# Both halves of a gated recurrence in one instruction each of tanh, decay, relu, gate, product and scan

## What is computed

```python
# recurrence: 256 inner features
hidden, gate = split(xn @ W_hg, 2)
z = sigmoid(gate);  a = 1 - z
h[t] = a[t] * h[t-1] + z[t] * (relu(hidden[t]) + 0.5)     # along each sequence
s = h @ W_out
# mixture of experts: a shared expert, and the best 2 of 16 routed ones
g = silu(shared(xn) + sum_k p_k * expert_k(xn))
out = x + s * g
```

## Time and profile before

| | us |
|---|---|
| median of 3 runs | 362.05 |
| the three runs | 361.15, 362.05, 365.03 |
| profiled execution, first to last instruction | 361.3 |
| TensorE busy | 304.3 (84%) |
| VectorE busy | 253.6 (70%) |
| ScalarE busy | 242.5 (67%) |
| GpSimd busy | 210.6 (58%) |

### The profile page before, as it was taken

The page is one execution under the profiler, slowest core; times in us unless marked ns, Lnnn a source line. Parts: engine busy times, 40 slices in busy tenths (PEclk is TensorE's granted clock), DMA queues, the critical chain, the costliest instruction groups (busy, mean ns, idle before and its releaser), DMA issues.

```text
span 361.3 us, 6017 instructions
## 1 busy us (share of the span) xinstructions
PE 304.3 (84%) x1532; PEld 197.9 (55%) x1532; DVE 253.6 (70%) x635; ACT 242.5 (67%) x518; POOL 210.6 (58%) x243
## 2 busy tenths in 40 slices
PE   0899999999979999995019879999999999999810
PEld 0457777766646666664015545656566666656510
DVE  7399999979998989795003457676767677676830
ACT  2789999988954788982026556767676776767410
POOL 4987544420137873777765646565656656565671
PEclk9999999999989999999557999999999999999975
DMA  8999996910003368333479624544645555520000
GB/s 241 289 406 412 416 437 236 427 66 0 3 22 133 135 225 324 114 150 138 156 239 402 263 86 124 173 130 131 184 151 147 149 146 153 150 76 17 15 0 1
DMA packets 27984, 63.82 MB, mean 177 GB/s; under 512 B 3701, under 2 KB 22784, under 8 KB 27056
## 3 DMA queue, kind: packets, MB, share of 16 engines
q1 hardware_dynamic: 20880, 45.78, 37.0%
q0 software_dynamic: 6784, 17.06, 12.7%
q10 hardware_dynamic: 288, 0.60, 0.5%
HBM read 29.52 MB, written 35.21 MB: 179 GB/s over the span
## 4 chain that ended last, share of the span: by engine, by line
PE 43%; issue 14%; POOL 14%; DVE 9%; ACT 8%; DMA 7%; another core or an unknown queue 2%; POOLq 0%; ACTq 0%; SPq 0%; DVEq 0%
PE p_u L976 13%; POOL slots L335 11%; PE p_u L903 8%; PE p_s L1001 8%; DMA slots<-arena,pos 5%; PE p_sh L988 3%; PE p_s L914 3%; PE p_lg L884 3%; ACT arena L444 2%; DVE rec L788 2%; PE p_xt L952 2%; POOL out L341 2%; DVE rec L780 1%; PE p_sh L923 1%
## 5 line engine op out<-in xcount | busy, mean ns | idle before, releaser
L341 POOL DMA_INDIRECT out<-arena x84 | 90.5, 1078 | 56.4 <-issue 40.1
L903 PE MATMUL p_u<-xT,w_front 128*128 128x512 f32 x192 | 92.3, 616 | 1.1 <-ACT xT L400 0.7
L335 POOL DMA_INDIRECT slots<-arena,pos x64 | 71.6, 1119 | 35.7 <-issue 17.9
L976 PE MATMUL p_u<-arena 128*128 x168 | 81.1, 606 | 0.0
L780 DVE TENSOR_TENSOR rec<-p_u,rec 128x512 f32<-128x512 f32 x42 | 29.0, 692 | 65.5 <-PE p_u L976 27.0
L1001 PEld LDWEIGHTS p_s<-arena,rec 128*128 128x128 f32 x336 | 40.9, 191 | 39.0 <-issue 38.9
L1001 PE MATMUL p_s<-arena,rec 128*128 x336 | 48.2, 286 | 6.7 <-ACT rec L464 3.0
L903 PEld LDWEIGHTS p_u<-xT,w_front 128*128 128x128 f32 x192 | 34.6, 195 | 33.5 <-issue 32.1
L444 ACT ACTIVATE arena<-arena 128x128 f32<-128x128 f32 x84 | 36.3, 480 | 14.8 <-DMA arena<-slots 14.8
L976 PEld LDWEIGHTS p_u<-arena 128*128 128x128 f32 x168 | 29.4, 196 | 20.7 <-issue 20.7
L543 DVE TENSOR_TENSOR_SCAN rec<-rec 128x512 f32<-128x512 f32 x32 | 39.2, 1225 | 1.1
(11 more groups left out here) (130 smaller groups left out, 433.0 us busy)
## 6 DMA issues: line engine op xcount, KB each, us to landing
slots<-arena SPq DMA_DIRECT2D x4, 4116.0 KB, 27.3
arena<-slots SPq DMA_DIRECT2D x42, 392.0 KB
arena<-in_W_lines SPq DMA_DIRECT2D x2, 2304.0 KB
arena<-in_x SPq DMA_DIRECT2D x16, 256.0 KB, 5.3
arena<-in_W_lines SPq DMA_DIRECT2D x1, 3072.0 KB
out<-arena POOLq DMA_INDIRECT x84
slots<-arena,pos POOLq DMA_INDIRECT x64
w_front<-in_W_front ACTq DMA_DIRECT2D x1, 392.0 KB, 3.5
```

Of the source, the lines that this page charges most:

```text
L335: pool.indirect_dma_start(slots, index, xrow[:, t], None).then_inc(s_disp[t % WINDOW], 16)
L341: pool.indirect_dma_start(out, index, xg[:, n % RX, h, X], None, bounds_check=T - 1, oob_is_err=False)\
L903: nc.tensor.matmul(p_u[:, n % 4], w_front[:, UPS[q]:UPS[q] + P], xT[:, c % XB], start=True, stop=True)\
L976: last = nc.tensor.matmul(p_u[:, n % 2 * 2 + h], xsT[:, n % 2, h * P:(h + 1) * P], w_lines[:, bass.DynSlice(line_at[2 * n + h], 4 * P)], s ...
```

## The change

The two halves of the inner features are handled together. `rec_in(c, j)`, called twice, becomes `rec_gates(c)` (tanh, then the decay a, each of both halves, 1024 columns) and `rec_hidden(c)` (relu, then the gate z). `rec_scan(c)` makes one product and one scan over 1024 columns; the zero decay at the start of each of the now four sequences still separates them. The projections are made in the order gate 0, gate 1, hidden 0, hidden 1, so that the two gates and the two hiddens lie in adjacent banks. The semaphores that counted halves count chunks. Nothing else changes.

```diff
@@ -223,7 +223,7 @@
 
         CONSTS = 17
         OFF_HG, OFF_S = E, E + 4 * P
-        UPS = [OFF_HG + 2 * P, OFF_HG, OFF_HG + 3 * P, OFF_HG + P, OFF_S, OFF_S + P]
+        UPS = [OFF_HG + 2 * P, OFF_HG + 3 * P, OFF_HG, OFF_HG + P, OFF_S, OFF_S + P]
 
         FIRST_TILES = FREE_CHUNKS * TT
         BLANK_BY_DVE = SLOTS // 8
@@ -399,21 +399,26 @@
                     act.wait_ge(s_up, NUP * (c - XB + 1))
                 nc.scalar.activation(xT[:, c % XB], p_xt[:, :], ACT.Copy).then_inc(s_xTe, 1)
 
-            def rec_in(c, j):
-                n = NH * c + j
-                act.wait_ge(s_up, NUP * c + 2 * j + 1)
+            def both(c, q):
+
+                return p_u[:, (NUP * c + q) % 4:(NUP * c + q) % 4 + NH]
+
+            def rec_gates(c):
+                act.wait_ge(s_up, NUP * c + 2)
                 if c >= 1:
-                    act.wait_ge(s_v, n - 1)
-                nc.scalar.activation(rec_z[:, j], p_u[:, (NUP * c + 2 * j) % 4], ACT.Tanh, scale=0.5).then_inc(s_tanh, 1)
-                act.wait_ge(s_up, NUP * c + 2 * j + 2)
+                    act.wait_ge(s_v, c)
+                nc.scalar.activation(rec_z, both(c, 0), ACT.Tanh, scale=0.5).then_inc(s_tanh, 1)
+                act.wait_ge(s_tanh, c + 1)
                 if c >= 1:
-                    act.wait_ge(s_scan, n - 1)
-                nc.scalar.activation(rec_v[:, j], p_u[:, (NUP * c + 2 * j + 1) % 4], ACT.Relu).then_inc(s_relu, 1)
-                act.wait_ge(s_tanh, n + 1)
-                halves = lambda a: a[:, j].rearrange("p (q n) -> p q n", q=2)[:, :, 1:]
+                    act.wait_ge(s_scan, c)
+                halves = lambda a: a.rearrange("p j (q n) -> p (j q) n", q=2)[:, :, 1:]
                 nc.scalar.activation(halves(rec_a), halves(rec_z), ACT.Copy, bias=0.5, scale=-0.5).then_inc(s_a, 1)
-                act.wait_ge(s_a, n + 1)
-                nc.scalar.activation(rec_z[:, j], rec_z[:, j], ACT.Copy, bias=0.5, scale=0.5).then_inc(s_z, 1)
+
+            def rec_hidden(c):
+                act.wait_ge(s_up, NUP * c + 2 * NH)
+                nc.scalar.activation(rec_v, both(c, NH), ACT.Relu).then_inc(s_relu, 1)
+                act.wait_ge(s_a, c + 1)
+                nc.scalar.activation(rec_z, rec_z, ACT.Copy, bias=0.5, scale=0.5).then_inc(s_z, 1)
 
             def shared_silu(c):
                 act.wait_ge(s_up, NUP * c + 5)
@@ -474,10 +479,10 @@
                 normalise(c)
             act.wait_ge(s_wfront, 16)
             for i in range(NCH):
-                rec_in(i, 0)
+                rec_gates(i)
                 for c in read(i)[:-1]:
                     copy_xT(c)
-                rec_in(i, 1)
+                rec_hidden(i)
                 for c in read(i)[-1:]:
                     copy_xT(c)
                 shared_silu(i)
@@ -530,18 +535,18 @@
                 nc.vector.tensor_copy(lg[:, a * TT:b * TT].rearrange("p t e -> p (t e)"), p_lg[:, 0:(b - a) * TT * E])\
                   .then_inc(s_lgc, b - a)
 
-            def rec_scan(c, j):
-                n = NH * c + j
-                dve.wait_ge(s_z, n + 1)
-                dve.wait_ge(s_relu, n + 1)
-                nc.vector.scalar_tensor_tensor(out=rec_v[:, j], in0=rec_v[:, j], scalar=0.5, in1=rec_z[:, j],
+            def rec_scan(c):
+                dve.wait_ge(s_z, c + 1)
+                dve.wait_ge(s_relu, c + 1)
+                nc.vector.scalar_tensor_tensor(out=rec_v, in0=rec_v, scalar=0.5, in1=rec_z,
                                                op0=ALU.add, op1=ALU.mult).then_inc(s_v, 1)
-                dve.wait_ge(s_v, n + 1)
-                dve.wait_ge(s_a, n + 1)
+                dve.wait_ge(s_v, c + 1)
+                dve.wait_ge(s_a, c + 1)
                 if c >= 2:
                     dve.wait_ge(s_ds, c - 1)
-                nc.vector.tensor_tensor_scan(rec_h[:, c % 2, j], rec_a[:, j], rec_v[:, j], 0.0, ALU.mult, ALU.add)\
-                  .then_inc(s_scan, 1)
+                nc.vector.tensor_tensor_scan(rec_h[:, c % 2].rearrange("p j n -> p (j n)"),
+                                             rec_a.rearrange("p j n -> p (j n)"), rec_v.rearrange("p j n -> p (j n)"),
+                                             0.0, ALU.mult, ALU.add).then_inc(s_scan, 1)
 
             def shared_gated(c):
                 dve.wait_ge(s_silu, c + 1)
@@ -837,10 +842,9 @@
                     positions(1, 0)
                 for c in STATS.get(i, []):
                     ln_stats(c)
-                rec_scan(i, 0)
+                rec_scan(i)
                 if i == 6:
                     route_keys(0)
-                rec_scan(i, 1)
                 if read(i):
                     copy_logits(read(i))
                 if i == 7:
@@ -892,10 +896,10 @@
                     pe.wait_ge(s_wfront, 16)
                 if n >= 4:
                     fc, fq = (n - 4) // NUP, (n - 4) % NUP
-                    if fq in (0, 2):
-                        pe.wait_ge(s_tanh, NH * fc + fq // 2 + 1)
-                    elif fq in (1, 3):
-                        pe.wait_ge(s_relu, NH * fc + fq // 2 + 1)
+                    if fq < NH:
+                        pe.wait_ge(s_tanh, fc + 1)
+                    elif fq < 2 * NH:
+                        pe.wait_ge(s_relu, fc + 1)
                     elif fq == 4:
                         pe.wait_ge(s_silu, fc + 1)
                     else:
@@ -904,7 +908,7 @@
                   .then_inc(s_up, 1)
 
             def rec_down(c):
-                pe.wait_ge(s_scan, NH * (c + 1))
+                pe.wait_ge(s_scan, c + 1)
                 if c == 0:
                     pe.wait_ge(s_wtail, 16)
                 if c >= 1:
@@ -966,7 +970,7 @@
                 pe.wait_ge(s_xsTe, n + 1)
                 if n == 0:
                     pe.wait_ge(s_lines, 48)
-                    pe.wait_ge(s_relu, NH * NCH)
+                    pe.wait_ge(s_relu, NCH)
                 elif n == 1:
                     pe.wait_ge(s_silu, NCH)
                     pe.wait_ge(s_gated, NCH)
```

## The result

The changed kernel takes 365.35 us (median of 14 runs, 364.8 to 368.5) against 363.55 us for the kernel before on the same chips (14 runs, 360.6 to 365.0). The ratio is 1.0081, 95% interval 1.0052 to 1.0110, which is 2.9 us (1.9 to 4.0) of 363.55. (That ratio isn't the ratio of the medians, which are only 1.8 us apart; the means are 2.7 us apart.) The forecast was +4.35 us, a ratio of 1.012: right in sign and mechanism, and outside the interval in size.

What follows compares the result with a forecast made beforehand. Bound taken as PE, then ACT and DVE, then POOL's 48 dispatches. Terms 0.2 + 1.15 + 3.0 = 4.35 us took the span from 361.3 to 365.65, median 366.4 us; range 362.4 to 368.6, forecast's own 364.5 to 368.3.

Steps and rivals of the forecast that it cites:

- What bounds: Chain on PE, then ACT and DVE, then POOL; recurrence acts only through positions at 104.14 us and 48 dispatches; cover 13.94 us.
- Durations: Times taken for 1024-column ops: scan 2.30, product 1.22, tanh and relu 1.01, a and z 1.05 us.
- Part 1: Stretch bound by PE, to about 82 us: relu waits for the fourth projection at the start; +0.2 us.
- Part 2: Chunks 6 to 8, on the path to the positions: DVE's first-half work no longer overlaps ACT; +1.15 us.
- The side remark on chunk 6: Chunk 6's lost overlap delays `shared_gated` by about 1 us and PE's fourth projection of chunk 7, but stays hidden.
- Part 3: POOL's 48 dispatches wait longer behind DVE's products and scans: +0.51 us a chunk, six chunks, +3.0 us.
- the second meeting: In a chunk after the change, POOL's next dispatch meets the scan 1.24 us in and waits 1.05 us.
- The first meeting: In a chunk after the change, POOL's first dispatch falls into the product (0.95 of cases) and waits 0.61 us.
- Stalls don't grow: Rival, chance 0.17: dispatch stalls cost 1.1 to 1.2 us a chunk as before; only 1.35 us is left, 363.4.
- Faster, per instruction: Rival, chance 0.06: a dispatch pays some 0.55 us per DVE instruction met, not its length; -2.0 us, 360.1.
- Worse: Rival, chance 0.08: dispatches slip between product and scan and wait 2.3 us a chunk; +8.1 us, 370.1.
- Nothing: Rival, chance 0.09: the start delay and the stalls are taken up; 362.05 us.

Runs made afterwards that it cites:

- after_again: The changed kernel profiled once more, nothing altered; 84.23 us from first double logits to the end of pos, 76.25 us from first to 48th dispatch.
- no67: Against the kernel before, halves handled together in all chunks but 6 and 7; ratio 1.0045 (1.0002 to 1.0089).
- the first pair: First profiles of the kernel before and the changed kernel, 82.73 and 83.88 us from first double logits to pos; the second pair profiles both again.
- the three profiles named above: Against the kernel before, halves joint in chunks 0 to 7 only (1.0029), in chunk 7 alone (73.44 us of dispatches), in all but 6 and 7 (1.0045).
- the quarters: Against the kernel before, DVE makes each half's product and scan in two pieces of 256 columns in chunks 8 to 15; ratio 1.0579 (1.0518 to 1.0639).

## Why the prediction was right, and where it was off

**What bounds.** Right. The change acted on the end through the two places named: when the positions are ready, and what happens to the 48 dispatches. Everything behind them in the first phase stayed covered: ACT's idle time before the second phase is 18.68 us in the profile after, against 13.94.

**Durations.** Scan 2.29 (taken: 2.30), product 1.22 (1.22), tanh and relu 1.00 to 1.02 (1.01), a and z 1.05 (1.05). The two widths of one exponential gave the slope of ACT to 0.01 us.

**Part 1, +0.2 us.** The wait was there in the profile after: PE idle 0.39 in place of 0.20, and all three profiles with chunk 0 joint and a late start have 0.39 to 0.45 where the five others with a late start have 0.19 or 0.20. In after_again, with its early start, PE had no such wait before the double logits, so there the term was 0. `no67` shows that chunks 1 to 5 add nothing. What the forecast missed was no part of the change: a start that comes some 2 us early or late by chance, more than most of the terms.

**Part 2, +1.15 us.** Measured 83.88 - 82.73 = 1.15 in the first pair, 1.5 in the second. The sum for chunk 7 came true in its parts: tanh at 90.89 and z's end at 94.83 in the profile after are 3.94 us apart (3.95 forecast). The side remark on chunk 6 was wrong: its lost overlap is not only a late shared product that stays hidden. It leaves DVE idle for 1.3 to 1.45 us before the product of chunk 6, nothing behind it takes that up, and by itself it costs as much as chunk 7. That the sum still came out is in part luck: the way that was left out happens to be 0.3 us shorter than the one that was followed.

**Part 3, +3.0 us: the term that was mis-sized.** It measured 76.4 - 74.75 = 1.7 us (1.3 without the three profiles named above). The rate of before was right: in chunks 8, 9, 10, 13, 14 and 15 the waits behind products and scans sum to 7.1 us in both profiles of before, 1.18 a chunk as worked out. Of the 1.69 forecast for the changed kernel, the second meeting is right, 1.00 us in every chunk of after_again but chunk 8 (1.05 forecast). The first meeting was taken as even over the product, 0.61 on average; it is 0.25 in chunk 8, then 0.94, 0.54, 0.12, 0.26 and 0.80. In chunk 8 the second is 0.77: there the phase is no chance at all, since POOL's first dispatch and DVE's product both start from `pos`. That is 8.7 us in both profiles of the changed kernel, 1.45 a chunk in place of 1.69, which over six chunks is 1.5 us, about the 1.3 that the term was too large by. The mean dispatch came out at 1199 and 1197 ns, not at the 1230 of the forecast.

**Sum.** 0.2 + 1.15 + 1.7 = 3.05 us, against 2.9 (1.9 to 4.0) measured; this closeness is better than the terms are known, each to some tenths of a us. With the term of the dispatches right, the forecast would have stood within the interval.

**The rivals.** "Stalls don't grow" is excluded by the waits of the six chunks, 8.7 us in both profiles of the changed kernel against 7.1 in both of the kernel before, and the stretch agrees: all four profiles with 1024 columns lie above all six with 512. "Faster, per instruction" is excluded by the same waits, which grew with half the instructions, and by the first 16 dispatches of the quarters. "Worse" asked for 2.3 us a chunk; the largest, in chunk 9, was 1.94. "Nothing" is excluded by both landmarks. Of the two rules weighed, that of the Trainium skill's "SBUF — State Buffer" (section "SBUF: two separate sides") on the pair held for a whole instruction was borne out (a dispatch that met a product or a scan ended 0.76 to 0.85 us behind that op's end, and only the first of the 48 ended 1.0 to 1.07 us behind, with pieces of 512 and 1024); that of "VectorE: DVE Perf Modes" (section on the TRN2 errata) on the fixed cost was true too (4.2 us less busy time on DVE) and without effect on the end.

## What to carry to other kernels

Joining two half-size instructions saved busy time on DVE and ACT here, and none of it reached the end, since neither engine bounded the stretches where it was saved. Where DVE used to start on the first half while ACT made the second, joining takes that overlap away, and in chunk 7 the overlap was worth 1.6 us against 0.4 saved. An instruction of DVE that reads two tiles also holds up each indirect transfer that GpSimd issues meanwhile, until its end: where GpSimd's transfers are the chain, look at the length of DVE's instructions, and not at their sum alone. And where two parts of a change are to be weighed at a few tenths of a per cent, compare distances between landmarks of several profiles, since a late start by chance can be larger than both. And when a run changes how much work one engine meets of another, as the waits of ACT did in the quarters, compare the waits for each piece of work met.

## What was not expected of the hardware

PE's matmuls ran at half speed from its first projection at about 12 us until 15 to 17 or until 19 to 22 us, at random from one execution to the next; the profile's row of granted clock says 1.00 there in both cases. At the first logits of two chunks the difference is some 2 us (3 in one profile), and PE, which bounds the next 60 us, doesn't make it up.

Shorter pieces on DVE, with which POOL's 48 dispatches need 72.7 in place of 74.75 us, went with waits of 8 to 20 us of ACT for nothing that the profile can name, and made the kernel 5.8% slower. No version tried is faster than the kernel before.
